# Opening of a gated attention and feed-forward block: who normalises the third and fourth row tile, and in what order the first context's and V weight's low halves are made

## What is computed

```python
x = x + tanh(g_xattn) * attention(layernorm(x), ctx, ctx)   # causal, one head of 512
x = x + tanh(g_ffn) * ffn(layernorm(x))

# attention: q = xn @ w_q; k = ctx @ w_k; v = ctx @ w_v
#            out = softmax(causal(q k^T / sqrt(512))) @ v
# ffn:       h = gelu(x @ ternary(W1)^T + b1);  out = h @ ternary(W2)^T + b2   (512 -> 2048 -> 512)
```

## Time and profile before

| | |
|---|---|
| median of 3 runs | 1585.43 (1584.88 to 1586.2) |
| the profiled execution | 1585.59, of which 1583.8 is the span from first to last instruction |
| TensorE busy | 1565.0, 99% of the span |
| VectorE, ScalarE, GpSimd busy | 1084.8 (68%), 817.4 (52%), 481.6 (30%) |
| TensorE's mean granted clock | 0.998 of full speed |

### The profile page before, as it was taken

How to read it: one execution, slowest core, us unless ns; L and a number is a source line. 1 busy time by engine, 2 the same in 40 slices (tenths; PEclk the granted TensorE clock), 3 DMA queues, 4 the chain that set the end, 5 groups by cost and what they waited for, 6 DMA issues and landing times.

```text
span 1583.8 us, 26069 instructions
## 1 busy us (share of the span) xinstructions
PE 1565.0 (99%) x10024; PEld 978.7 (62%) x10024; DVE 1084.8 (68%) x1821; ACT 817.4 (52%) x1454; POOL 481.6 (30%) x468
## 2 busy tenths in 40 slices
PE   7899999999999999999999999999999999999998
PEld 4556555565656565565666666666666666666665
DVE  6766656577787778766577667766766676767664
ACT  4334444433233333334666666666666666666654
POOL 5211111111111111134244444334533453445330
PEclk9999999999999999999999999999999999999999
DMA  7447667655655665553322242323333242324210
GB/s 213 129 105 190 152 177 157 179 131 121 164 133 164 138 163 140 131 130 79 81 77 77 62 86 79 83 71 68 84 88 77 53 101 77 77 47 100 51 51 27
DMA packets 307964, 170.81 MB, mean 108 GB/s; under 512 B 268208, under 2 KB 268224, under 8 KB 306688
## 3 DMA queue, kind: packets, MB, share of 16 engines
q1 hardware_dynamic: 306368, 166.52, 43.1%
q10 hardware_dynamic: 1296, 2.36, 0.4%
q0 software_dynamic: 176, 0.27, 0.1%
HBM read 70.53 MB, written 33.55 MB: 66 GB/s over the span
## 4 chain that ended last, share of the span: by engine, by line
PE 95%; DMA 2%; DVE 2%; issue 1%; ACT 1%; SPq 0%; POOL 0%; DVEq 0%
PE s_ps L1265 14%; PE e_ps L1265 14%; PE s_ps L1330 11%; PE o_ps L1360 11%; PE v_ps L1311 10%; PE t_ps L1292 10%; PE o_ps L1209 7%; PE t_ps L1209 7%; PE v_ps L1209 7%; PE m_ps L1209 3%; DMA raw<-in_ctxT 1%; DMA ctx_s<-in_wqT 0%; PE e_ps L1360 0%; PE e_ps L1292 0%; DVE ctx_s L773 0%
## 5 line engine op out<-in xcount | busy, mean ns | idle before, releaser
L1071 DVE SCALAR_TENSOR_TENSOR v_s<-xnT,sc,v_s 128x512 f16<-128x512 f32 x256 | 239.4, 956 | 106.5 <-ACT v_s L698 106.5
L691 ACT ACTIVATE xnT<-tT,b_s 128x256 f32<-128x256 f32 x384 | 173.9, 499 | 179.0 <-DVE tT L1059 63.0
L1265 PE MATMUL s_ps<-w_s,v_s 128*128 128x512 f16 x1024 | 263.0, 380 | 0.0
L1265 PE MATMUL e_ps<-w_s,v_s 128*128 128x512 f16 x1024 | 262.9, 379 | 0.0
L574 ACT ACTIVATE p<-s_ps,ebias,esc 128x128 f32<-128x128 f32 (+3 forms) x64 | 53.2, 831 | 340.8 <-DVE ebias L930 340.8
L1330 PE MATMUL s_ps<-ctx_s,tT 128*128 128x512 f16 (+3 forms) x1152 | 197.7, 326 | 4.3 <-DVE tT L888 3.6
L1360 PE MATMUL o_ps<-v_s,pT 128*128 128x512 f16 x840 | 191.6, 379 | 0.0
L698 ACT ACTIVATE v_s<-xnT,sc 128x512 f16<-128x512 f32 x256 | 176.3, 712 | 7.5
L1311 PE MATMUL v_ps<-wv_s,ctx_s 128*128 128x512 f16 x768 | 176.2, 380 | 0.8 <-DVE v_s L895 0.8
L1265 PEld LDWEIGHTS e_ps<-w_s,v_s 128*128 128x128 f16 x1024 | 100.2, 98 | 120.8
L1292 PE MATMUL t_ps<-xnT,a_s 128*128 128x256 f16 x1488 | 172.8, 273 | 0.1
(11 more groups left out here) (179 smaller groups left out, 2404.0 us busy)
## 6 DMA issues: line engine op xcount, KB each, us to landing
out_y<-x_ring SPq DMA_DIRECT2D x128, 256.0 KB, 2.2
x_ring<-in_x SPq DMA_DIRECT2D x63, 256.0 KB, 2.9
raw<-in_ctxT SPq DMA_DIRECT2D x7, 2048.0 KB, 7.9
raw<-out_y SPq DMA_DIRECT2D x44, 256.0 KB, 3.8
w_in<-in_w1T SPq DMA_DIRECT2D x16, 512.0 KB, 3.9
w_in<-in_w2T SPq DMA_DIRECT2D x16, 512.0 KB, 3.9
x_ring<-out_y SPq DMA_DIRECT2D x20, 256.0 KB, 3.7
xnT<-xn_both SPq DMA_TRANSPOSE x128, 2.5
```

The source lines that it names most:

```text
L691: a.activation(g32n[:, j, half * 2 * P:(half + 1) * 2 * P], src, ACT.Gelu, bias=b1_s[:, f:f + 1], scale=1.0 / YN).then_inc(g_act, 1)
L1071: v.scalar_tensor_tensor(out=g_s[:, U % 2, j, LO], in0=g32n[:, j], scalar=col(C_SG), in1=g_s[:, U % 2, j, HI], op0=ALU.mult, op1=ALU.subtr ...
L1265: last_mm = mm(y_ps[i], g_s[:, U % 2, j, a, i * P:(i + 1) * P], w2_s[:, f, :], start=(U % UG == 0 and n == 0 and a == HI), stop=(U % UG == ...
```

## The change

Row tiles 2 and 3 are normalised by VectorE (`first_rows(2)` and `first_rows(3)`, now in its own program, the second between the two halves of `product_lower`). GpSimd keeps their `rstd` and LO: both `rstd` first, then both LO. ScalarE makes tile 3's HI ahead of both `ctx_bound` and the first quarter of the context's HI ahead of the two `t_upper`. VectorE makes the context's scale, the V weight's LO and the first quarter of the context's LO ahead of both `t_lower`, and `first_stats(4)` behind them.

```diff
@@ gpsimd
-            first_rows(2)
-            first_rows(3)
+            first_scale(2)
+            first_scale(3)
+            first_low(2)
+            first_low(3)
             g.dma_start(b2_row[:, :], b2.partition_broadcast(P)).then_inc(b2_in, 16)
             first_rows(4)
+            def first_scale(k):
+                r = k % 2
+                pool.wait_ge(ln_var, k + 1)
+                g.tensor_tensor(rstd[:, r:r + 1], var_s[:, r:r + 1], minus_half[:, :], ALU.pow).then_inc(ln_rstd, 1)
+            def first_low(k):
+                r = k % 2
+                pool.wait_ge(xn_hi, k + 1)
+                pool.wait_ge(x_turned[r], turned_before(0, k - LN_LEAD))
+                g.tensor_tensor(xn_s[:, r, LO], xn32[:, r], xn_s[:, r, HI], ALU.subtract).then_inc(xn_lo, 1)
@@ scalar
+            rows_upper(0, -2)
             ctx_bound(0)
-            rows_upper(0, -2)
             ctx_bound(1)
...
+            ctx_upper(0, 0, 0)
             t_upper(0, -2)
             t_upper(0, -1)
...
-            ctx_upper(0, 0, 0)
             ctx_upper(0, 0, 1)
@@ vector
             scale_product()
+            first_rows(2)
             first_stats(3)
             dve.wait_ge(consts, 6)
             wv_max()
-            product_lower()
+            product_lower((0, 1))
+            first_rows(3)
+            product_lower((2, 3))
             scale_wv()
             ctx_diagonal(0)
-            t_lower(0, -2)
             scale_first_ctx()
-            first_stats(4)
             wv_lower()
             ctx_lower(0, 0, 0)
+            t_lower(0, -2)
             t_lower(0, -1)
+            first_stats(4)
             v_lower(0, -1)
```

More of the change, by code:

```diff
@@ L795, in scale_product, with product_lower @@
                                 ALU.mult).then_inc(a_scaled, 1)
-            def product_lower():
-                for m in range(DC):
+            def product_lower(ms):
+                for m in ms:
                     dve.wait_ge(a_hi, m + 1)
@@ L908, in first_rows @@
             def first_rows(k):
-                ln_rows(k, k % 2, x_ring[:, k], False)
+                ln_rows(k, k % 2, x_ring[:, k], k >= 2)
             def slot(it, s, last=False):
```

## The result

The changed kernel takes 1588.01 us in the median (22 runs, 1585.81 to 1590.73), the kernel before 1585.21 in 22 runs beside it. The ratio is 1.0019 with a 95% interval of 1.0012 to 1.0025: 2.8 us slower, where 1.9 less was forecast, and outside the range of the prediction (1580.8 to 1586.1). By the bound of 0.2% this is still "no change", but the interval excludes both nothing and the forecast. The profiled execution took 1588.65, 3.06 more than the one of before.

The account below looks back on a forecast made before the run. TensorE's wait for tile 3's turned rows before `t_product(0, 0)` was taken as the bound. Its start 1.9 earlier, with nothing gained or lost elsewhere, gave 1585.43 - 1.9 = 1583.5 us; range of 8 in 10: 1580.8 to 1586.1.

Parts of the forecast that it names:

- What bounds the kernel: Opening before 80 us: TensorE waits 4.1 us for `xnT` ahead of `t_product(0, 0)`; savings there last to the end.
- Tile 3 earlier: Tile 3's rows on VectorE, HI and LO after: LO ready near 24.5 instead of 27.64, 3.1 earlier.
- What that is worth in the queue: SyncE's queue: tile 3's turns land at 31.5 instead of 33.3, so TensorE starts at 31.6, 1.9 earlier.
- Tile 3's turns land right behind tile 2's, 0.5 apart: SyncE's queue: tile 2 lands at 30.7 and 31.2, tile 3 at 31.7 and 32.2.
- the empty us can go: DMA engines, all but empty from 29 to 30: without that us tile 3 lands at 31.2.
- `b2_row` earlier: GpSimd's load moves from 27.58 to about 24.6 and delays the turns by 0.3, bounds 0 to 1.5.
- The clock: TensorE at `t_product(0, 0)`: the clock still falls, so the product takes 5.07 and ends at 36.7 instead of 38.55.
- The low halves: Ahead of `v_product(0, -1)`: the context's LO ends at 34.4 instead of 37.3, hidden by the slow product; no gain.
- (b): Tile 4's `rstd` and rows on GpSimd move back, ready at about 39.5; slot 0 at 42.7 leaves 3.2 of cover.
- The queue gives nothing: Rival on SyncE's queue: tile 3 lands within half a us of 33.3; time 1585.1, chance 0.12.
- The slower rival: `b2_row` goes ahead of the turns on the shared DMA engines, 25 to 31: up to 1.5 slower, 1586.9; chance 0.06.
- the first of the conditions for being wrong: Sign in the trace after: the prediction is wrong if the turns land at 33 or later.

Follow-up runs that it names:

- `b2_row` last: Load of `b2_row` issued behind tile 4's rows in GpSimd's `first_rows`, in either kernel: changed kernel 1584.65 (0.9996), kernel before 1584.41 (0.9995).
- the turns first: SyncE issues tiles 2 and 3's turns ahead of row tiles 4 to 6's loads, `b2_row` last: kernel before 1583.27, changed kernel 1581.27.
- early rows alone: Changed kernel with the low halves in the order of before: 1587.85 (1.0015).
- the last kernel: Changed kernel with the turns first, plus tile 4's rows on VectorE and `b2_row` between GpSimd's `rstd` and LO of tile 4: 1580.25 (0.9968).

## Why the prediction was wrong

**What bounds the kernel.** Right in that the wait for tile 3's turns is the bound, and that what the opening lost at 38.55 arrived unchanged at the end (3.01 of 3.06). What the wait is made of was read only in part (below).

**Tile 3 earlier.** Right in every step: 24.5 forecast, 24.4 measured less the start. The four operations did what the earlier trace rows said.

**What that is worth in the queue: the step that failed.** It had three terms, and the runs split the loss between them. With `b2_row` at its old time the changed kernel gains nothing: 1585.85 against 1585.25 beside it, and a wait in the queue of 15.02 against 14.67. The forecast had taken 2.1 for turns that land at 31.2 instead of 33.3. The earlier `b2_row` then costs 2.2, where 0.3 was taken.

- *Tile 3's turns land right behind tile 2's, 0.5 apart.* Right where nothing mixes: 31.65 and 32.15 with `b2_row` last, against "31.7 and 32.2".
- *"the empty us can go".* Wrong. It stayed: share 0.31 and 7 GB/s in 30 to 31, and 27 packets in 29 to 30 without `b2_row`. It does not come from the long issue either: with the turns first in the changed kernel no issue of these turns took over 1.36 us, and the silence was there.
- *`b2_row` earlier: "I take 0.3, nearer to 0", bounds 0 to 1.5.* This is the term that made the kernel slower. Moved from 27.6 to 25.7 the load cost 2.2 us, above the upper bound, which priced it by its bytes alone. Against `b2_row` last it cost 3.4. The rows that should have warned were there: in the earlier trace rows tile 2's turns landed at 30.7 and 31.2 but tile 3's, beside `b2_row`, only at 33.34, 3.46 after an issue. The prediction read those 2 us as the long issue at 27.73 and the empty us.

The missing gain has a cause of its own. LO of tile 3 ready 3.1 earlier was worth nothing by itself: with `b2_row` last, the kernel before has its last turn at a wait of 13.26, the changed kernel at 13.38, and their times are 1584.41 and 1584.65. In the former, the turns issued at 27.5 and 28.75 still came in time, the last landing 3.03 after its issue. The queue was the bound, not LO. Of the 2.1 us from 31.2 to 33.3, for which the prediction had the late LO and the empty us, 1.4 were the cost of `b2_row` beside the turns (14.67 less 13.26).

The Trainium skill, "DMA: Bandwidth & Descriptors", section "Issuing engines are not separate DMA queues", has transfers of all issuing engines interleave on the same 16 engines. The trace agrees, and q0 beside q1 above is the picture of it. As the prediction applied it, a price of bytes, it gave a landing at 32.7. Measured less the start: 35.6.

**The clock.** It fell as forecast, but it was back at 2.4 GHz 0.9 us ahead of the product's end instead of 0.4, so the product took 4.52, not 5.07. That softened the loss by 0.55.

**The low halves.** Right: the context's LO ended at 35.72, less the start 34.4, as forecast, and was hidden (early rows alone 1587.85, the whole change 1588.01). It is worth 1.3 only where the turns come earlier.

**What moves back.** (b) Tile 4's rows were ready at 40.76, less the start 39.4, against 39.5, and slot 0 found them there. With VectorE idle beside them, `rstd` took 0.56 and the rows 2.08 where the earlier trace rows has 2.59 and 2.62. By the Trainium skill, "SBUF — State Buffer", section "Who interferes with whom", a VectorE instruction with two inputs in SBUF needs the read port that it shares with GpSimd, and one of the two waits. The trace agrees, also with the 3.00 above.

**Rivals.** "The queue gives nothing" (0.12) describes the first half of what happened: with `b2_row` at its old time tile 3's last turn landed at a wait of 15.02, 0.35 from before. The slower rival had the right place and cause, `b2_row` on the shared engines, but its price was "up to 1.5", and with it the chance was set at 0.06. Of what was named, the first of the conditions for being wrong came true: the turns landed at 33 or later.

## What to carry to other kernels

A load moved forward is not free because its bytes "had to be moved anyway": ask which transfer of the critical path will be in flight when it gets its turn, and put it behind that one, in the same queue if need be. Turns through the DMA engines are the ones to keep alone: beside a second queue they fell to 49 to 306 packets in a us where the mix was worst (418 to 495 where it was mild), alone they did up to 1079. When a producer is made earlier and its consumer stands in a full queue, change the order of the queue first: here that was worth 1.1 us in the kernel before and 3.4 in the changed one (which in the traces includes a product of 2.78 at the fast clock instead of 5.28), the producer alone nothing.

## What the runs showed of the hardware

- The load that GpSimd issued while SyncE's queue was full did not start with its issue. Issued at 25.69, it moved from 31.4 on, and before, issued at 27.58, from 30.5. With the queue empty (`b2_row` last, issued at 39.6) it moved from 40.9 on. Issued from ScalarE's queue at 22.6 it moved from 26.0 on and landed at 29.2.
- Among the turns there is about a us in which next to nothing moves, with `b2_row` early or last: 21 to 77 packets in that us in ten of the traces. It does not stand between the last loads and the first turns, as the prediction had it. In the kernel before 619 of the turns' 2048 packets of 256 bytes have gone by 28.8, and the silence follows. With the turns first in the changed kernel 1519 have gone by 27.9, so it stands ahead of the last turn and of all three row tiles. SyncE's long issues (2.11 before, up to 3.50 after) are not needed for it. Its cause is open; none of the runs removed it.
- The clock is not settled by the idle time alone. With the turns first, in the kernel before, TensorE started at 31.99 and kept 2.4 GHz. In the last kernel it started at 30.83, after 0.56 of idle time instead of 1.98, and fell to 1.2 GHz in 31 to 32 (mean 0.71), which made the product 1.7 us longer. One kernel seems to do both: of the eleven runs of the kernel before with the turns first and the changed order of the low halves, three have a mean clock of 1.000 and take 1580.4 to 1580.9, the other eight 1581.6 to 1584.4.
- The landing of the first weights scatters by over 1 us with the same code (7.3 to 9.1 us after the issue in the traces), and in the pair of before and after the difference is still there at the end.
